# Cross-attention and a routed feed-forward on one core: the part behind the loop placed in both paths and split, and some early jobs reordered

## What is computed

```
x = x + attention(layernorm(x), ctx)        # 16 heads of 8, 1024 queries, 6404 keys
    q = n @ Wq + bq; k = ctx @ Wk + bk; v = ctx @ Wv + bv
    softmax(clip(q k^T / sqrt(8), -1e4, 1e4)) v, then @ Wo + bo
x = x + ffn(layernorm(x))
    main   = gelu(n @ W1m + b1m) @ W2m + b2m                  # hidden 512
    logits = mean over rows(n) @ w_gate + b_gate              # 8 experts
    probs  = softmax(logits); the two largest, divided by their sum, are the experts' weights
    out    = a * main + (1 - a) * sum_k weight_k * expert_k(n),   a = clip(alpha, 0.1, 1)
```

## Time and profile before

| | |
|---|---|
| three runs, us | 785.46, 785.53, 788.52 (median 785.53) |
| the profiled execution, us | 788.86, its span 786.9 |
| mean granted TensorE clock in it | 0.993 |
| PE busy | 733.3 us, 93% |
| ACT busy | 718.1 us, 91% |
| DVE busy | 564.5 us, 72% |
| POOL busy | 28.8 us, 4% |

### The profile page before, as it was taken

The page is one execution under the profiler, slowest core; times in us unless marked ns, Lnnn a source line. Parts: engine busy times, 40 slices in busy tenths (PEclk is TensorE's granted clock), DMA queues, the critical chain, the costliest instruction groups (busy, mean ns, idle before and its releaser), DMA issues.

```text
span 786.9 us, 13292 instructions
## 1 busy us (share of the span) xinstructions
PE 733.3 (93%) x5412; PEld 219.2 (28%) x5412; DVE 564.5 (72%) x789; ACT 718.1 (91%) x574; POOL 28.8 (4%) x50
## 2 busy tenths in 40 slices
PE   6999989999999999999999999999999999999898
PEld 3534322222222222222222222222222222222457
DVE  6944178798878978797788897897789773139320
ACT  4868999999999999999999999999999999999351
POOL 5240000000000000000000000000000000000000
PEclk9979999999999999999999999999999999999999
DMA  5678100011110000111100000111100000000010
GB/s 163 203 179 254 31 1 1 21 47 35 34 35 1 2 0 2 34 37 49 51 2 1 1 1 18 45 41 35 34 1 1 1 1 2 1 1 1 2 55 27
DMA packets 18043, 28.53 MB, mean 36 GB/s; under 512 B 5286, under 2 KB 8732, under 8 KB 17980
## 3 DMA queue, kind: packets, MB, share of 16 engines
q1 hardware_dynamic: 12730, 23.71, 10.1%
q0 software_dynamic: 4032, 3.30, 1.8%
q10 hardware_dynamic: 1218, 0.64, 0.3%
HBM read 19.50 MB, written 8.13 MB: 35 GB/s over the span
## 4 chain that ended last, share of the span: by engine, by line
PE 58%; ACT 19%; issue 16%; DVE 3%; DMA 2%; POOLq 0%; SPq 0%; POOL 0%; ACTq 0%
PE po L1232 31%; PE ps L1147 17%; ACT region_ctx L533 14%; ACT probs_own L533 5%; PE ps L1327 2%; PE po L1048 2%; DMA k_dram<-kparts 1%; PE po L1337 1%; PE po L1218 1%; PE ps L1037 1%; DVE pT L632 1%; PE po L1147 1%; DMA xres<-in_x 1%; PE po L1124 1%; DMA region_ctx<-in_w1e 0%
## 5 line engine op out<-in xcount | busy, mean ns | idle before, releaser
L533 ACT ACTIVATE region_ctx<-ps 128x1536 f32<-128x1536 f32 x375 | 528.5, 1512 | 12.7 <-PE ps L1147 12.4
L1232 PE MATMUL po<-region_ctx,v 128*9 128x512 f32 x2238 | 392.0, 598 | 0.5 <-ACT region_ctx L533 0.5
L1147 PE MATMUL ps<-qst,region_k 32*128 32x512 f32 x1492 | 251.1, 493 | 36.6 <-ACT region_ctx L533 26.3
L1147 PEld LDWEIGHTS ps<-qst,region_k 32*128 32x128 f32 x1492 | 96.5, 182 | 408.3 <-ACT region_ctx L533 289.9
L1232 PE MATMUL po<-probs_own,v 128*9 128x512 f32 x746 | 192.9, 598 | 0.5 <-ACT region_ctx L533 0.5
L533 ACT ACTIVATE probs_own<-ps 128x1536 f32<-128x1536 f32 x125 | 189.1, 1513 | 3.3 <-PE ps L1147 2.9
L840 DVE TENSOR_SCALAR region_kT<-po 128x512 f32<-128x512 f32 x108 | 74.1, 686 | 86.1 <-PE po L1147 86.1
L843 DVE SCALAR_TENSOR_TENSOR region_kT<-region_kT,po 128x512 f32<-128x512 f32 x108 | 73.5, 680 | 0.3
L881 DVE SCALAR_TENSOR_TENSOR dres<-region_kT,dres 128x1024 f32<-128x1024 f32 x54 | 66.1, 1225 | 1.7
L878 DVE SCALAR_TENSOR_TENSOR dres<-region_kT,dres 128x1024 f32<-128x1024 f32 x54 | 65.8, 1218 | 0.2
L870 DVE SCALAR_TENSOR_TENSOR dres<-region_kT 128x1024 f32<-128x1024 f32 x54 | 65.8, 1218 | 0.0
(11 more groups left out here) (216 smaller groups left out, 352.4 us busy)
## 6 DMA issues: line engine op xcount, KB each, us to landing
region_k<-k_dram SPq DMA_DIRECT2D x40, 320.0 KB, 3.3
k_dram<-kparts SPq DMA_DIRECT2D x18, 320.0 KB, 4.2
qst<-q_dram POOLq DMA_DIRECT2D x12, 128.0 KB, 9.9
region_ctx<-in_ctx SPq DMA_DIRECT2D x2, 624.0 KB, 9.4
q_dram<-dres POOLq DMA_DIRECT2D x2, 512.0 KB, 3.1
k_dram<-kparts SPq DMA_DIRECT2D x2, 322.0 KB, 3.6
region_ctx<-in_ctx SPq DMA_DIRECT2D x1, 576.0 KB, 7.8
xres<-in_x SPq DMA_DIRECT2D x1, 512.0 KB, 4.4
```

What stands on the lines that cost most here:

```text
L533: act.activation(probs_of(t), ps[t % NSB][:, :], ACT.Exp, scale=ESCALE).then_inc(exp_ready, 1)
L1147: return mm(dst, kst[r, kt * P:(kt + 1) * P], qst[r, g, queries], start=True, stop=True)
L1232: last = mm(dst[QUAD * j:QUAD * j + V9, :], w, src, start=first, stop=last_one, skip_group_check=True)
```

## The change

- **Front.** PE scores tile 1 ahead of V chunk 1. DVE takes V chunks 0 and 1 one behind the other, ahead of the key bounds. The second half of q is picked behind the first bound job's result, and q is split behind the second one's, both in `take_job`.
- **D_PLAN.** The last value step is due at tile 498, not 499.
- **Both paths.** What stood behind the conditional is now a function `behind_loop` on ACT, DVE and PE, called at the end of `If` and at the end of `Else`.
- **Pieces.** For the second half of the queries, the sums, the normalised rows, their transposes, the projection and the residual go in two pieces of 256 columns each, in PSUM banks of their own; `second_main` is cut into single matmuls that stand between them. `IDLE` is 3.
- **Root.** The second half's variance goes to ACT (`Sqrt`, with a table switch ahead of it and one back to gelu behind it) and four DVE operations (`refine`), not to POOL. `xn_transpose` waits tile by tile.
- **Gate.** The two largest are taken from the logits, and only their exponentials relative to the largest are used; six operations between logits and index become two. The main path's second layer for the second half goes block by block over the hidden dimension.

```diff
-            for n in range(NHALF):
-                pool.wait_ge(var_ready, 2 + n)
...
+            pool.wait_ge(var_ready, 2)
+            pool.tensor_tensor(rstd[:, 3, 0:QT // 2], rstd[:, 0, 0:QT // 2], powers[:, 0:QT // 2], ALU.pow).then_inc(std_ready, 1)
...
+            def behind_loop():
+                act.wait_ge(pre_taken, CB)
+                act.activation(hid[0][:, :, 0:BANK], pre[:, :, :], ACT.Gelu_apprx_tanh).then_inc(main0_ready, 1)
+                act.wait_ge(table_step, 2)
+                act.activation(scratch[:, :], ones[0:1, 0:1], ACT.Sqrt).then_inc(table_step, 1)
+                act.wait_ge(var_ready, 3)
+                act.activation(rstd[:, 1, QT // 2:QT], rstd[:, 0, QT // 2:QT], ACT.Sqrt).then_inc(std_ready, 1)
+                act.wait_ge(table_step, 3)
+                act.activation(scratch[:, :], ones[0:1, 0:1], ACT.Gelu_apprx_tanh).then_inc(table_step, 1)
...
-                if c == 6:
-                    pick_q(1)
...
-            dve.wait_ge(v_psum, 1)
-            take_v(0, po[0]).then_inc(v_done, 1)
+            for c in range(2):
+                dve.wait_ge(v_psum, c + 1)
+                take_v(c, po[c]).then_inc(v_done, 1)
...
-            dve.wait_ge(v_psum, 2)
-            take_v(1, po[1]).then_inc(v_done, 1)
...
-            split_q()
...
                     v.tensor_reduce(gcol[:, i:i + 1], src[0:2 * H, :], AX.X, ALU.max).then_inc(spare_taken, 1)
+                    if i == 0:
+                        pick_q(1)
+                    else:
+                        split_q()
...
+                refine(halves[1], 3, tlink)
+                scale_rows(halves[1])
...
+                tlink(v.scalar_tensor_tensor(gate[0:1, 0, :], po[1][0:1, 0:E], 1.0 / NQ, bg[:, :], ALU.mult, ALU.add))
+                tlink(v.max(gate[0:1, 6, :], gate[0:1, 0, :]))
+                v.max_index(topi[:, :], gate[0:1, 6, :], gate[0:1, 0, :]).then_inc(topk_ready, 1)
+                v.tensor_scalar(gate[0:1, 1, :], gate[0:1, 6, :], gate[0:1, 6, 0:1], None, ALU.subtract).then_inc(msum_ready, 1)
+                dve.wait_ge(exp_gate, 1)
...
+                for a in range(2):
+                    cols = slice(a * PAIR, (a + 1) * PAIR)
+                    v.tensor_copy(oraw[:, (NP - 1) % 2, cols], po[pv_bank(NP - 1)][:, cols]).then_inc(o_taken, 1)
+                for a in range(2):
+                    dve.wait_ge(tok_psum, a + 1)
+                    normalise(NP - 1, bank(a, P, PAIR),
+                              slice(QT // 2 + 2 * a, QT // 2 + 2 * a + 2)).then_inc(attention_done, NHALF if a == 0 else 1)
                 second_half_residual(flink)
+                behind_loop()
...
-            project_v(1, po[1]).then_inc(v_psum, 1)
             pe.wait_ge(k_ready, KCH)
             score_tile(1)
+            project_v(1, po[1]).then_inc(v_psum, 1)
...
+                second_main(range(0, 2))
+                att_transpose_piece(0)
+                att_transpose_piece(1)
+                second_main(range(2, 3))
+                project_out_piece(0)
+                project_out_piece(1)
+                second_main(range(3, CB * QT // 2))
+                behind_loop()
...
+                for cb in range(CB):
+                    pe.wait_ge(hid_ready, cb + 1)
+                    for t in range(QT // 2, QT):
+                        dst, first = ffn_sum(t)
+                        last = mm(dst, hid[0][:, cb, t * P:(t + 1) * P], w2m_sb[:, cb, :], start=(cb == 0 and first), stop=False,
+                                  skip_group_check=True)
```

More of the change, by code:

```diff
@@ L595, in statistics, with variance @@
                     last = v.bn_stats(stats[:, t, :], xres[:, t, :])
+                variance(tiles, last, link)
+            def variance(tiles, last, link):
                 link(last)
@@ L623, in _ @@
             statistics(range(QT), link)
-            refine(range(QT), link)
+            refine(range(QT), 1, link)
             scale_rows(range(QT))
@@ L759, in second_half_residual @@
             def second_half_residual(link):
-                dve.wait_ge(attT_psum, NHALF)
-                v.tensor_copy(attT[:, BANK:NQ], bank(4)).then_inc(attT_ready, 1)
-                residual(1, bank(5), link)
+                for a in range(2):
+                    dve.wait_ge(attT_psum, NHALF + a)
+                    v.tensor_copy(attT[:, BANK + a * PAIR:BANK + (a + 1) * PAIR], bank((4, 1)[a], P, PAIR)).then_inc(attT_ready, 1)
+                for a in range(2):
+                    r = slice(halves[1].start + 2 * a, halves[1].start + 2 * a + 2)
+                    dve.wait_ge(y_psum, NHALF + a)
+                    v.tensor_tensor(xres[:, r, :], bank((5, 2)[a], P, PAIR).rearrange("p (t c) -> p t c", c=C), xres[:, r, :],
+                                    ALU.add).then_inc(y_taken, 1)
+                    dve.wait_ge(y_taken, NHALF + a)
+                    for t in range(r.start, r.stop):
+                        last = v.bn_stats(stats[:, t, :], xres[:, t, :])
+                variance(halves[1], last, link)
             def first_half_main(link):
@@ L984, in _ @@
-            v.tensor_scalar(mix[0:1, 1:3], gate[0:1, 6, 0:TOPK], gate[0:1, 4, 3:4], gate[0:1, 7, 0:1], ALU.mult, ALU.mult).then_inc(mix_ready, 1)
-            dve.wait_ge(topk_ready, 1)
-            for e in range(TOPK):
-                i = dve.value_load(topi[0:1, e:e + 1], min_val=0, max_val=E - 1)
-                last = v.tensor_copy(b1s[:, e, :], b1T[:, bass.ds(i * CB, CB)])
-            last.then_inc(b1s_ready, 1)
-            dve.wait_ge(mixb_psum, 1)
-            v.tensor_copy(mixb[:, 1:3], bank(MIX_BANK)[:, 0:TOPK]).then_inc(mixb_taken, 1)
@@ L1330, in second_layer @@
-            def second_layer(e, half):
-                pe.wait_ge(hid_ready, e * CB * NHALF + CB * half)
-                pe.wait_ge(w2_scaled, e + 1)
-                w2 = w2m_sb if e == 0 else w2s[:, e - 1, :, :]
-                for t in range(half * QT // 2, (half + 1) * QT // 2):
-                    dst, first = ffn_sum(t)
-                    for cb in range(CB):
-                        last = mm(dst, hid[e % 2][:, cb, t * P:(t + 1) * P], w2[:, cb, :],
-                                  start=(e == 0 and cb == 0 and first), stop=(e == TOPK and cb == CB - 1), skip_group_check=True)
-                    if e == TOPK and any(t == t1 - 1 for _, t1 in OUT_TILES):
-                        last.then_inc(ffn_psum, 1)
-                if e < TOPK and half == 1:
-                    last.then_inc(ffn2_done, 1)
@@ L1364, in _ @@
-            for e in range(1, TOPK + 1):
-                for half in range(NHALF):
-                    second_layer(e, half)
+                for a in range(2):
+                    att_transpose_piece(a)
+                for a in range(2):
+                    project_out_piece(a)
+                second_main(range(CB * QT // 2))
+                behind_loop()
 _OUT = ((1, NQ, C), "float32")
```

233 lines of the change are left out of this document (134 added, 99 removed), and 2 rows, old and new, of the table D_PLAN.

## The result

The changed kernel takes 777.13 us (median of four runs, 776.76 to 777.34), the kernel before beside it 786.58 (four runs, 785.46 to 788.52). The ratio is 0.9872, with a 95% interval of 0.9846 to 0.9899: 1.3% faster. The forecast was 775.7, its range 773.3 to 781.0.

A forecast was written before the change was run, and what follows sets the result against it. ACT and PE bound the kernel, so gains come only ahead of tile 36 and behind the last exponential. 7.4 + 0.4 + 1.2 + 1.55 + 0.3 + 2.75 - 0.4 = 13.2 off 788.86 gives 775.7 us, range 773.3 to 781.0.

The forecast's parts named there:

- PE's idle time at the start: Ahead of tile 36: scoring tile 1 before V chunk 1 shrinks PE's idle time from 2.2 to some 0.3 us, earning 1.9.
- The clock: From 38.9 to 49.1 us: with PE's gap gone the granted clock stays at 1.0, not 0.50, earning 4.6 us.
- the stall: At 66.1 us: PE no longer idles behind a split of K waiting for a K store, earning 0.9 us.
- Moving q's split: On DVE in the front: q's split behind bound job 1 costs nothing; without cover at most 2 us.
- The count of 91.0: Ahead of tile 36: PE's 56.4 us of work, counted from 34.62, ends at 91.0; the trace had tile 36 at 98.58.
- the pieces: Tail, from the end of the values to the variance: working in two pieces overlaps the stages, earning 1.2 us.
- The jump: Tail, variance to first scaled tile: no jump out of the conditional there, 1.15 us against 2.70, earning 1.55.
- The gate: Tail, logits to index: fewer operations make index and weights' DMA earlier, and all 2.75 us count.
- (a): Rival: the clock falls all the same, for the same 10.2 us, giving 780.3; chance 0.12.
- (b): Rival: the front earns nothing against the median and only the tail's 5.8 us count, giving 779.7; chance 0.12.
- (c): Rival: DVE doesn't wait for the jump or it returns fully, and the gate's gain meets PE: 778.6; chance 0.08.
- (d): Rival: with three idle matmuls the clock falls near 740 and stays down to the end, giving 805; chance 0.02.

The follow-up runs named there:

- the filled kernel: The kernel before with six unread 128x128 matmuls put behind tile 2's scores, where PE was idle: 783.91 us, ratio 0.996.
- the tail alone: The changed kernel with the order ahead of tile 36 as before and only the tail changed: 781.87 us, ratio to before 0.994.
- the q-early kernel: The changed kernel with q's second half picked and q split ahead of the loop, as before: 778.36 us, ratio 0.9883.
- the old gate: The changed kernel with the gate as before, softmax over all eight, then the two largest and the index: 778.91 us, ratio 0.9894.
- the front alone: The kernel before with only the work ahead of tile 36 changed: 782.28 us, ratio 0.9934.
- the merged kernels: The changed kernel with `behind_loop` called once, behind the conditional: 781.50 us with three unread matmuls, 779.30 with ten.
- V's order old: The changed kernel with V chunk 1 ahead of tile 1's scores and taken behind the key bounds, as before: 779.91 us, ratio 0.990.

## Why the prediction held, step by step

**Bound.** The forecast put the gain in two places and nothing between. The loop's row is the same in both traces. Right. The price of a tile in it was read too high: 465 exponentials in 632 us are 1.36 us each, not 1.38 to 1.40; no term of the sum hangs on it.

**PE's idle time at the start, 1.9.** 1.70 measured, as the distance of tile 36 between the filled kernel and the changed one. By PE's own gaps it is 1.8: 1.41 and 0.50 us in before, 0.11 left in the changed kernel. Right in cause and nearly in size.

**The clock, 4.6, and the stall, 0.9.** The cause was right, and argued from one trace only; the filled kernel shows it. The size: tile 36 at 98.58 in before's profiled execution and 93.66 in the filled one, with tile 0 starting 0.14 later: 5.1 for both terms, forecast 5.5. The tiles part the two: up to tile 16 (66.51 and 62.49) it is 4.2, and the other 0.9 comes between tiles 16 and 20, where the stall is. So the clock was taken 0.4 to 0.5 us too large, and the stall at its size. The reason given for the stall is not shown. With q early a split waits for a store 2.06 us in before, 0.34 with the tail alone and 1.54 in the q-early kernel, and not at all in the filled one; with q late it waits in several kernels too, 1.75 us with the old gate. PE is late by such a wait in before's trace alone. Why the store took 10.9 us there was not tried by itself.

**Moving q's split, "cost nothing".** It was the other way round. Left early behind a faster start, the split stands in front of DVE's take of V chunk 2 and makes PE wait 1.17 us. The move pays 1.2 us, and this is the part of the front whose purpose the prediction didn't see. In before there was room for it, since PE was late itself.

**The count of 91.0.** It came to 91.96. PE's windows from its first V projection to the end of tile 36's scores, in before and in the changed kernel:

```profile
34.62:98.54 63.92, 60.31 (x430) 24.35 (x431) 25.99 (x60) 50.70 (x38) 9.32 (x21) 0.92 0.59 167
```

```profile
34.76:91.91 57.15, 56.22 (x430) 23.27 (x431) 26.92 (x61) 50.71 (x38) 9.59 (x21) 1.00 0.62 180
```

The work was counted rightly: 56.2 us measured, 56.4 forecast, the estimate of 1.7 for the four other jobs with it. The step that failed is "this is all that is lost there". PE waits for an exponential three more times, 0.8 us together, in both kernels:

```profile
64.57 0.50 PE L1197 MATMUL ps<-qst,region_k 32*128 32x512 f32 x3 [0.23 <-ACT region_ctx L533]
...
78.75 0.51 PE L1197 MATMUL ps<-qst,region_k 32*128 32x512 f32 x3 [0.34 <-ACT region_ctx L533]
...
83.40 0.50 PE L1197 MATMUL ps<-qst,region_k 32*128 32x512 f32 x3 [0.24 <-ACT region_ctx L533]
```

In before they stand at 71.21, 85.39 and 90.03. The count closed on before's trace because the half clock was taken too large: by PE's busy time, 60.3 and 56.2, it cost 4.1 us and not 4.6. Of the front's miss, 7.4 against 6.6, the clock is 0.5, the idle time 0.1 and the later start of the changed execution 0.14.

**The last D step, 0.4; the pieces, 1.2; transposing tile by tile, 0.3.** 0.6, 1.3 and 0.3. Most of the pieces' profit is where it was worked out, in the overlap from the second transposes on; 0.2 of it is there at the second normalising already, where the prediction had nothing.

**The jump, 1.55.** 1.6 by the traces. The experiment says what the before trace left open: all of it is the jump. The root on ACT in place of POOL's power earns 0.04. Of the table load the row shows 1.28 us (732.24) and the dummy activation behind it over at 733.73, with the transposes done at 734.57: hidden by 0.8, forecast 0.9. The Trainium skill (ScalarE: Activation LUTs, What ACT_TABLE_LOAD costs) counts a drain of about 1.38 us besides; the load here starts 0.02 us behind the root's end, so no run here shows that drain, and the 0.5 us that it would have cost by the prediction's estimate did not come.

**The gate, 2.75.** The largest miss: 1.6 measured for the whole stage. The index came 2.8 us earlier as forecast, and the weights landed 3.8 us earlier: SP's load, now issued 2.1 us ahead of ACT's and not together with it, took 2.9 us and not 3.93. What failed is the sentence on what is late next. It had PE's second layer end 0.97 us behind the fourth hidden block. That would need PE to have done the first three blocks by then, and PE only comes to the first at 739.2 to 739.4, when the first layer's matmuls are through; 32 instructions at 0.11 are 3.6 us from there, and 742.95 is where it ends. Against the DMA's 741.0 the bound had changed to PE, and from ACT's copy on PE has no gap to the end. The prediction looked at the inputs of the last block and not at the engine's own queue.

**The jump at the end, -0.4.** -0.52.

**The rivals.** (a) did not happen in the changed kernel, whose four runs have clocks of 0.999 and 1.0; in the traces of the three kernels with the old order and the gap left open it does. (b) falls with the front alone. (c) falls with the merged kernels, but for its last part: the gate's gain did meet PE, and 1.1 of the 2.75 us went there. (d) was not this kernel's, but its mechanism is real: with three unread matmuls and the jump kept, the clock falls at 735.5. It came back after 6.9 us and cost about 2, not 29. So the two edits, jump out and `IDLE` to 3, belong together. The wrong number of unread matmuls loses either way: ten without the jump 1.0 us, three with it 2.2.

The sum of 13.2 against the traces' 11.6 is 1.1 too much at the gate, 0.8 in the front, and 0.3 too little in the small terms.

The forecast of the time missed by 1.4 us. The gain by the medians, 9.5 against 9.8, agrees better than that by luck: before's median rose from 785.53 to 786.58 with the fourth run, and against the first three the gain is 8.4. Right in the prediction, and not luck, is that the changed kernel comes out the same from either kind of before's runs, since what differs between those runs is gone from it. The lower end of the range was added up wrongly: 775.7 less 0.5, 0.4, 0.3 and 1 is 773.5, not 773.3.

## What to carry to other kernels

When a wait ahead of an engine is shortened, ask for the engine's own queue first: how much it still has to issue before the instruction in question, and when it can begin. A count of an engine's work must be checked against its gaps one by one, or a term that is too large hides gaps that were left out. A gap of 1.4 us on PE cost 4.1 us here through the clock, and whether it does changes from run to run; a spread of the times that goes with the mean granted clock is the sign, and a few unread matmuls in the gap are the test. The end of a conditional held DVE up for nearly 3 us here, so a critical chain should not cross it. POOL's power seemed to be part of that wait; moving it to another engine earned nothing, because the jump was the whole of it.

## What the runs showed of the hardware that was not expected

- One and the same program, the kernel before, ran in 783.7 to 784.3 us where its mean clock was 1.0, in 785.2 to 788.0 at 0.996, and once in 793.95 at 0.989. Only the first kind of run matches the kernel with the gap filled.
- Falls of different lengths in one kernel family: 10.2 us (38.9 to 49.1) in before, 3.4 (41.2 to 44.6) with the tail alone, 6.8 (39.8 to 46.7) with V's order old.
- The chosen expert's 256 KB of first weights land in 3.9 us where ACT's queue issues its own loads at the same time (3.6 with the old gate), and in 2.9 where these come 2.1 us later.
- From DVE's last instruction inside the conditional to its next one behind it are 2.9 us at three places in these traces (from 740.40 in before, 731.80 in the merged kernel and 772.12 at the end of the changed one), and on PE 1.4 and 1.5 us of idle time show at the first two.
